# Self attention of a two-layer diffusion block: a pair addition of 128x2048 on GpSimd written as four additions of 128x512, with TensorE waiting for them head by head

## The chip, the cores and the metric

One core of one Trainium2 chip runs the whole program. The metric is the device time of one execution in microseconds (us). PE is TensorE, PEld its weight loads, DVE VectorE, ACT ScalarE, POOL GpSimd and SP the engine that issues most DMAs.

## The reference, cut to what matters

The input is `x` of 8 batches with 512 tokens of 512 features. Layer L0 adds a cross attention to a context of 77 tokens. Layer L1 adds a self attention, a second cross attention and an MLP with a hidden size of 2048. There are 16 heads of 32 features, all in float32. The change lies in the self attention:

```
attn_w = softmax(einsum('bhqd,bhkd->bhqk', q, k) * scale, axis=-1)
attn_out = einsum('bhqk,bhkd->bhqd', attn_w, v)   # then heads side by side
x = x + gate_a * (attn_out @ W_proj + b_proj)
```

## The kernel before, in words

The stages follow one another: preparation, cross attention L0, the products for queries, keys and values, self attention, the second cross attention, the MLP. Each engine has its own list of instructions, and semaphores tie the lists together. Steps of several loops are woven into one list by `braid`, so the order on each engine is fixed when the program is built.

The self attention works on 32 groups n, one for each batch and each set of four heads. In a group, `attend` makes the scores with keys on the partitions: 4 key tiles (kt) times 4 heads, one matmul each (L1901). ScalarE writes the exponential of each score tile (L1979) into `self_exponentials`, four buffers `p[0]` to `p[3]` of 128 x 4 heads x 512 queries in float32. TensorE then does two things with them. `values` (L1923) multiplies each `p[kt]` with the values, four matmuls with 32 columns, one for each head, into the four 32-partition strips of one bank. `sum_pair` (L1935) multiplies with a matrix of ones in the same four strips and gives the denominators. To halve those sums GpSimd first adds `p[1]` into `p[0]`, and `p[3]` into `p[2]` (L1781). So there are two additions for a group, 64 in all, and 64 calls of `sum_pair`.

TensorE asks for the sums late: `sum_pair(n, 0)` is called just before the values of kt 3, in the second step of the next group, and `sum_pair(n, 1)` just before the values of kt 1 of the next group. ScalarE may overwrite `p[0]` and `p[2]` only after the sums have read them (L1971, L1972).

Between these, TensorE makes the scores once more with queries on the partitions for group n+2 (L1880). VectorE takes the negated maximum of each (L1815), TensorE turns the maxima (L1889), and they go back as rows of the query stack. These maxima use three banks, so TensorE waits for VectorE when it is late. VectorE also does `finish` for the group before: it turns the sums (L1829), inverts them (L1832), spreads them (L1835), multiplies the heads (L1841: two inputs in SBUF) and takes the low part (L1846: two inputs in SBUF). In the groups 0 to 3 VectorE splits one piece of the projection weights as well (L266: `weight_stage` minus its high part, two inputs in SBUF). GpSimd adds the residual base (L1764) and the gated rows (L1790) for the batch before, tiles of 128x512.

From the group 27 on, steps of the second cross attention are woven in: its normalisation (L312, L321), transposes (L354) and the splits of its weights (L266).

A wait on TensorE is carried by the weight load of the matmul that follows it. `Port` leaves out a wait for a value that the engine has waited for already. In the cross attentions `values` has the four value matmuls (L1332), then a wait for VectorE's `sums_turned` of the group before, then the four sum matmuls (L1339).

Of the kernel before, what the change touches and what calls it, by code (L numbers as in the profile page):

```python
# [7 lines left out]
ALU = mybir.AluOpType  # L8
# [7 lines left out]
GH = P // HD  # L16
# [35 lines left out]
def s_at(kb):  # L52
    return S_AT + int(kb * KB)


class Done:


    def __init__(self, sem, base, by):
        self.sem, self.base, self.by = sem, base, by  # L60
# [1553 lines left out]
class SelfAttention:  # L1614
# [4 lines left out]
    def __init__(self, k, w, x_in, x_out, wp):  # L1619
        self.k, self.w, self.x_in, self.x_out, self.wp = k, w, x_in, x_out, wp  # L1620
        n, c = LAST, k.count
        self.key_ones = c("vector_self_key_ones", 4)
        self.q_fetched, self.k_fetched = k.slots("self_query_stack", 4, n, 3), k.slots("self_key_stack", 4, n, 3)
        self.v_loaded = k.slots("self_values", 3, n)
        self.smax, self.negmax = c("tensor_scores_for_max", n * GH * NT), c("vector_negated_maxima", n * GH * NT)
        self.rows_turned = c("tensor_turned_maxima", n)
        self.row_hi, self.row_lo = c("scalar_max_row_hi", n), c("vector_max_row_lo", n)
        self.rows_put = k.slots("self_max_rows", 4, n, 2)
        self.score, self.exp = c("tensor_scores_by_key", n * NT * GH), c("scalar_exponentials", n * NT * GH)
        self.av, self.summed = c("tensor_value_sums", n * NT), c("tensor_exponential_sums", n * 2)  # L1630
        self.paired = c("pool_exponential_pairs", n * 2)
        self.heads_copied, self.heads_hi = c("scalar_heads_float32", n), c("scalar_heads_hi", n)
        self.sums_turned, self.inverted = c("vector_sums_turned", n), c("vector_reciprocals", n)
        self.spread, self.normalised = c("vector_reciprocals_spread", n), c("vector_normalised_heads", n)
        self.heads_lo = c("vector_heads_lo", n)
        self.x_loaded, self.x_stored = c("dma_x_rows", B, 16), c("dma_x_out", B, 16)
        self.gate_loaded = c("dma_self_gate", B, 32)
        self.based, self.projected = c("pool_residual_bases", B * NT), c("tensor_projections", B * NT)
        self.gated, self.added = c("vector_gated_rows", B * NT), c("pool_residuals", B * NT)
        self.scores, self.max_banks, self.products = k.ring(0, 1), k.ring(2, 3, 4), k.ring(5)  # L1640
        self.heads, self.sums = k.ring(6), k.ring(7)
        self.q = [k.at(f"self_query_stack{i}", [ST_MAX, GH, N], s_at(at), F32R) for i, at in enumerate((0, 16, 80, 48))]
        self.keys = [k.at(f"self_key_stack{i}", [ST_MAX, GH, N], s_at(at + 8), F32R) for i, at in enumerate((0, 16, 80, 48))]
        self.p = [k.at(f"self_exponentials{i}", [P, GH, N], s_at(at)) for i, at in enumerate((32, 40, 64, 72))]
        self.w_p = k.pair("self_w_p", [P, KC, D], s_at(96), s_at(104))
        self.v = [k.at(f"self_values{i}", [P, NT, P], at) for i, at in enumerate((s_at(114), s_at(112), OUTS + 8 * KB))]
        self.gated_rows = k.at("self_gated_rows", [P, D], OUTS + 10 * KB)
        self.gate = k.at("self_gate_and_bias", [P, 2, D], WIDE)
# [108 lines left out]
    def gpsimd(self, e, pool):  # L1757
        k = self.k

        def add_base(b):  # L1760
            pool.wait_ge(*self.x_loaded(b))
            pool.wait_ge(*self.gate_loaded(b))
            for t in range(NT):
                e.tensor_tensor(k.x[:, t, :], k.x[:, t, :], self.gate[:, 1, :], ALU.add).then_inc(self.based.sem, 1)  # L1764

        def attend(n):
            for kt in range(NT):
                for h in range(GH):
                    yield
                    if h == 1:  # L1770
                        if kt:
                            values(n, kt - 1)
                        elif n:
                            values(n - 1, NT - 1)

        def values(n, kt):
            if kt % 2 == 0:
                return
            pool.wait_ge(*self.exp((n * NT + kt) * GH + GH - 1))
            pool.wait_ge(*self.av(n * NT + kt - 1))  # L1780
            e.tensor_tensor(self.p[kt - 1][:], self.p[kt - 1][:], self.p[kt][:], ALU.add).then_inc(self.paired.sem, 1)  # L1781

        def project(b):
            for t in range(NT):
                i = b * NT + t
                for _ in range(3):
                    yield
                pool.wait_ge(*self.gated(i))
                pool.wait_ge(*self.based(i))
                e.tensor_tensor(k.x[:, t, :], self.gated_rows[:], k.x[:, t, :], ALU.add).then_inc(self.added.sem, 1)  # L1790
                yield

        return SelfSteps(add_base=add_base, attend=attend, project=project, values=values)

    def vector(self, e, dve):
# [71 lines left out]
    def tensor(self, e, pe):  # L1867
# [59 lines left out]
        def sum_pair(n, j):  # L1927
            if j == 0:
                _, before = self.sums.take(("sums", n), self.sums_turned(n))
                if before:  # L1930
                    pe.wait_ge(*before)
            bk = self.sums.of["sums", n]
            pe.wait_ge(*self.paired(2 * n + j))
            for h in range(GH):
                mm = e.matmul(k.bank[h * HD:(h + 1) * HD, bk, :], k.ones[:], self.p[2 * j][:, h, :],  # L1935
                              start=j == 0, stop=j == 1)
            mm.then_inc(self.summed.sem, 1)

        def project(b):
            for t in range(NT):  # L1940
# [9 lines left out]
                yield  # L1950

        return SelfSteps(maxima=maxima, max_rows=max_rows, attend=attend, project=project, values=values, sum_pair=sum_pair)

    def scalar(self, e, act):
        k = self.k

        def max_rows(n):
            act.wait_ge(*self.rows_turned(n))
            if n >= 2:
                act.wait_ge(*self.rows_put(n - 2))  # L1960
            else:
                for done in self.freed_rows:
                    act.wait_ge(*done)
            e.activation(k.mr[n % 2][:, 0, :], k.bank[0:GH * NT, self.max_banks.of["rows", n], 0:P],
                         ACT.Copy).then_inc(self.row_hi.sem, 1)
            yield

        def attend(n):
            for kt in range(NT):
                if n > 0:  # L1970
                    act.wait_ge(*self.paired(2 * (n - 1) + kt // 2))  # L1971
                    act.wait_ge(*(self.av((n - 1) * NT + kt) if kt % 2 else self.summed(2 * (n - 1) + kt // 2)))  # L1972
                else:
                    for done in self.freed_p[kt // 2]:
                        act.wait_ge(*done)
                for h in range(GH):
                    i = (n * NT + kt) * GH + h
                    act.wait_ge(*self.score(i))
                    e.activation(self.p[kt][:, h, :], k.bank[:, self.scores.of["score", i], :], ACT.Exp,  # L1979
                                 scale=SCALE).then_inc(self.exp.sem, 1)  # L1980
                    yield

        def finish(n):
            yield
            yield
            act.wait_ge(*self.av(n * NT + NT - 1))
            if n >= 2:
                act.wait_ge(*self.heads_lo(n - 2))
            else:
                for done in self.freed_wide:  # L1990
                    act.wait_ge(*done)
            e.copy(k.o_wide[n % 2][:], k.bank[:, self.heads.of["heads", n], :]).then_inc(self.heads_copied.sem, 1)
            for _ in range(12):
                yield
            act.wait_ge(*self.normalised(n))
            if n >= 6:
                act.wait_ge(*self.projected(((n - 6) // G) * NT + NT - 1))
            else:
                for done in self.freed_o:
                    act.wait_ge(*done)  # L2000
            e.copy(k.o[n % 6][:, 0, :], k.o_wide[n % 2][:]).then_inc(self.heads_hi.sem, 1)
            yield

        return SelfSteps(lambda p: self.w.split_hi(e, act, p), max_rows=max_rows, attend=attend, finish=finish)


# [390 lines left out]
```

## Time and profile before

| | |
|---|---|
| median of three runs | 2545.93 us (2542.42 to 2553.8) |
| the profiled execution | 2551.88 us, its span 2550.1 us |
| PE busy | 2408.3 us, 94% of the span |
| DVE busy | 1390.8 us, 55% |
| ACT busy | 1025.2 us, 40% |
| POOL busy | 582.4 us, 23% |
| L1781 busy | 294.5 us in 64 instructions, mean 4602 ns |
| self attention | from about 822 to about 1476 us of the span |

Busy time of an engine is the union of its instructions. An idle time is put down to the instruction whose semaphore ended it, or to "issue" where no semaphore did. A float32 matmul stands in the trace as two matmuls, two passes of one instruction. So one `sum_pair` gives eight L1935 matmuls.

### The profile page before, as it was taken

To read this page: it belongs to the slowest core of one execution; us is meant where nothing else is said; L and a number is where in the kernel's file an instruction comes from. 1 tells how busy PE (TensorE), PEld (TensorE's weight loads), DVE (VectorE), ACT (ScalarE), POOL (GpSimd) and SP (SyncE) were. 2 spreads that over 40 slices of the span, in tenths; PEclk is the share of its full clock that TensorE was granted. 3 is DMA by queue.
4 is the path that set the end of the run, shared out by engine and by line. 5 is a ranking of instruction groups with operands and counts; after the bars stand their busy time and mean duration, and the time that the engine had idled before them with its cause. 6 is when DMAs were issued, how large, how long until landed. Compare 5 with 4: busy or idle time off the path is not lost.

```text
span 2550.1 us, 32330 instructions
## 1 busy us (share of the span) xinstructions
PE 2408.3 (94%) x12048; PEld 1688.5 (66%) x12048; DVE 1390.8 (55%) x2463; ACT 1025.2 (40%) x1831; POOL 582.4 (23%) x325
## 2 busy tenths in 40 slices
PE   6889999999999899999998789999999999999999
PEld 5656666578877344444444457667588888888887
DVE  4566666654456777877777457666643222322221
ACT  3444444433322555555554334444442322233232
POOL 2101211210000466666665412111211011101100
PEclk9889999999999899999999899999999999999999
DMA  6687767555574546565553478787431101110110
GB/s 209 188 208 225 210 188 216 174 168 194 190 239 150 120 114 157 138 149 136 124 148 92 127 184 218 202 222 194 153 108 58 58 1 58 58 51 7 58 42 17
DMA packets 261323, 354.19 MB, mean 139 GB/s; under 512 B 61027, under 2 KB 109243, under 8 KB 261166
## 3 DMA queue, kind: packets, MB, share of 16 engines
q1 hardware_dynamic: 259998, 348.27, 48.4%
q0 software_dynamic: 1168, 3.85, 0.4%
q8 instruction: 96, 1.57, 0.3%
q14 instruction: 61, 0.50, 0.1%
HBM read 233.78 MB, written 116.69 MB: 137 GB/s over the span
## 4 chain that ended last, share of the span: by engine, by line
PE 81%; DVE 7%; ACT 4%; issue 3%; DMA 3%; SPq 1%; POOL 1%; DVEq 0%; ACTq 0%; POOLq 0%
PE banks L396 43%; PE banks L2195 14%; PE banks L1901 6%; PE banks L1923 4%; PE banks L1880 4%; PE banks L1935 2%; PE banks L1318 2%; PE banks L1332 2%; PE banks L1339 2%; PE banks L354 2%; DMA norm_x<-x 1%; ACT wide L377 1%; DVE negated_max L1815 1%; DVE norm_x L321 1%; PE banks L765 1%
## 5 line engine op out<-in xcount | busy, mean ns | idle before, releaser
L1979 ACT ACTIVATE self_exponentials<-banks 128x512 f32<-128x512 f32 x512 | 286.4, 594 | 291.2 <-PE banks L1935 138.7
L1815 DVE TENSOR_REDUCE negated_max<-banks 128x1 f32<-128x512 f32 x512 | 329.9, 677 | 100.4 <-PE banks L1880 98.9
L1781 POOL TENSOR_TENSOR self_exponentials<-self_exponentials,self_exponentials 128x2048 f32<-128x2048 f32 x64 | 294.5, 4602 | 202.5 <-ACT self_exponentials L1979 202.5
L2195 PE MATMUL banks<-mlp_w_down_hi,out_parts 128*128 128x512 f32 x1024 | 333.8, 389 | 0.1
L337 POOL TENSOR_SCALAR norm_rstd<-norm_mean_var 128x4 f32<-128x4 f32 x32 | 8.0, 249 | 1341.3 <-DVE norm_mean_var L316 1341.3
L2152 DVE TENSOR_TENSOR out_parts<-wide,out_parts 128x512 fp32r<-128x512 f32 x128 | 93.0, 727 | 371.2 <-ACT out_parts L2224 371.2
L2214 ACT ACTIVATE wide<-banks,bias_columns 128x512 f32<-128x512 f32 x128 | 88.3, 690 | 426.0 <-PE banks L396 426.0
L1901 PE MATMUL banks<-self_query_stack,self_key_stack 98*128 98x512 f32 x512 | 233.3, 457 | 7.8 <-ACT self_exponentials L1979 4.9
L1901 PEld LDWEIGHTS banks<-self_query_stack,self_key_stack 98*128 98x128 f32 x512 | 97.6, 191 | 185.9 <-ACT self_exponentials L1979 147.3
L2195 PEld LDWEIGHTS banks<-mlp_w_down_hi,out_parts 128*128 128x128 f32 x1024 | 192.2, 188 | 40.5 <-DVE cross_last_x_rows L1261 0.5
L1880 PE MATMUL banks<-self_key_stack,self_query_stack 96*128 96x512 f32 x512 | 208.6, 411 | 6.3 <-DVE negated_max L1815 5.1
L2195 PE MATMUL banks<-mlp_w_down_lo,out_parts 128*128 128x512 f32 x512 | 199.2, 389 | 0.0
L1217 DVE TENSOR_REDUCE negated_max<-banks 128x4 f32<-128x308 f32 x256 | 121.1, 473 | 107.7 <-PE banks L396 104.0
L1923 PE MATMUL banks<-self_exponentials,self_values 128*32 128x512 f32 x1024 | 138.3, 612 | 0.7 <-ACT self_exponentials L1979 0.7
L1400 ACT ACTIVATE cross_exponentials<-banks 77x512 f32<-77x512 f32 x128 | 75.6, 592 | 111.7 <-PE banks L1318 111.6
L377 ACT ACTIVATE wide<-banks,modulation_columns 128x512 f32<-128x512 f32 x96 | 74.5, 776 | 108.8 <-PE banks L354 102.0
L1880 PEld LDWEIGHTS banks<-self_key_stack,self_query_stack 96*128 96x128 f32 x512 | 98.8, 193 | 25.3 <-DVE negated_max L1815 12.3
L312 DVE BATCH_NORM_STATS2 norm_stats<-norm_x 128x6 f32<-128x512 f32 x128 | 84.6, 671 | 53.7 <-DMA norm_x<-x 53.7
L1400 ACT ACTIVATE L_exponentials<-banks 77x512 f32<-77x512 f32 x128 | 75.3, 591 | 91.3 <-PE banks L1318 91.3
L2195 PEld LDWEIGHTS banks<-mlp_w_down_lo,out_parts 128*128 128x128 f32 x512 | 96.1, 188 | 19.9
L1592 ACT ACTIVATE out_parts<-banks,bias_columns 128x512 fp32r<-128x512 f32 x64 | 44.1, 689 | 161.3 <-PE banks L396 134.8
L329 DVE TENSOR_TENSOR x_lo<-wide,x_hi 128x512 fp32r<-128x512 f32 x80 | 56.3, 704 | 94.0 <-ACT x_hi L379 93.8
(208 smaller groups left out, 5323.6 us busy)
## 6 DMA issues: line engine op xcount, KB each, us to landing
L_query_stack<-q_parts_L SPq DMA_DIRECT2D x96, 256.0 KB, 4.9
norm_x<-x SPq DMA_DIRECT2D x24, 1024.0 KB, 7.5
self_query_stack<-q_parts_self SPq DMA_DIRECT2D x96, 256.0 KB, 4.1
self_key_stack<-k_parts_self SPq DMA_DIRECT2D x96, 256.0 KB, 6.3
cross_query_stack<-q_parts_cross SPq DMA_DIRECT2D x96, 256.0 KB, 4.9
x_rows<-x SPq DMA_DIRECT2D x23, 1024.0 KB, 5.9
x<-x_rows SPq DMA_DIRECT2D x22, 1024.0 KB, 5.0
q_parts_L<-out_parts SPq DMA_DIRECT2D x32, 512.0 KB, 3.7
```

Source lines behind the costliest of these rows:

```text
L377: e.activation(k.wides[w][:], bank, ACT.Identity, **kw).then_inc(self.wide.sem, 1)
L396: mm = e.matmul(out_ap, l, r, start=i == 0, stop=i == len(terms) - 1)
L1217: e.tensor_reduce(k.nm[n % 2][:, t:GH * NT:NT], k.bank[:, bk, 0:GH * S].rearrange("p (h k) -> p h k", k=S), AX_X, ALU.max, negate=True).th ...
L1400: e.activation(self.p[:, i % self.HEADS_KEPT, :], k.bank[0:S, self.scores.of["score", i], :], ACT.Exp, scale=SCALE).then_inc(self.exp.sem, 1)
L1781: e.tensor_tensor(self.p[kt - 1][:], self.p[kt - 1][:], self.p[kt][:], ALU.add).then_inc(self.paired.sem, 1)
L1815: e.tensor_reduce(k.nm[n % 2][:, h * NT + t:h * NT + t + 1], k.bank[:, self.max_banks.of["max", i], :], AX_X, ALU.max, negate=True).then_i ...
L1880: e.matmul(k.bank[:, bk, :], self.q[n % 4][0:ST, h, t * P:(t + 1) * P], self.keys[n % 4][0:ST, h, :], start=True, stop=True).then_inc(self ...
L1901: e.matmul(k.bank[:, bk, :], self.keys[n % 4][0:ST_MAX, h, kt * P:(kt + 1) * P], self.q[n % 4][0:ST_MAX, h, :], start=True, stop=True).the ...
L1923: mm = e.matmul(k.bank[h * HD:(h + 1) * HD, bk, :], self.v[n % 3][:, kt, h * HD:(h + 1) * HD], self.p[kt][:, h, :], start=kt == 0, stop=kt ...
L1979: e.activation(self.p[kt][:, h, :], k.bank[:, self.scores.of["score", i], :], ACT.Exp, scale=SCALE).then_inc(self.exp.sem, 1)
L2152: e.tensor_tensor(h[:, 1, :], k.wides[k.wide_turns.of["up", i]][:], raw(h[:, 0, :]), ALU.subtract).then_inc(self.lo.sem, 1)
L2195: mm = e.matmul(bank, l, w, start=j == 0 and q == 0, stop=j == JC - 1 and q == 2)
```

## The change

GpSimd's one addition over all four heads becomes four, one for each head, each with an increment of the same semaphore. TensorE's one wait ahead of the four sum matmuls becomes a wait ahead of each. ScalarE's wait is moved to the new count and still asks for the last head.

```diff
-        self.paired = c("pool_exponential_pairs", n * 2)
+        self.paired = c("pool_exponential_pairs", n * 2 * GH)
...
             pool.wait_ge(*self.exp((n * NT + kt) * GH + GH - 1))
             pool.wait_ge(*self.av(n * NT + kt - 1))
-            e.tensor_tensor(self.p[kt - 1][:], self.p[kt - 1][:], self.p[kt][:], ALU.add).then_inc(self.paired.sem, 1)
+            for h in range(GH):
+                e.tensor_tensor(self.p[kt - 1][:, h, :], self.p[kt - 1][:, h, :], self.p[kt][:, h, :],
+                                ALU.add).then_inc(self.paired.sem, 1)
...
-            pe.wait_ge(*self.paired(2 * n + j))
             for h in range(GH):
+                pe.wait_ge(*self.paired((2 * n + j) * GH + h))
                 mm = e.matmul(k.bank[h * HD:(h + 1) * HD, bk, :], k.ones[:], self.p[2 * j][:, h, :],
                               start=j == 0, stop=j == 1)
...
-                    act.wait_ge(*self.paired(2 * (n - 1) + kt // 2))
+                    act.wait_ge(*self.paired((2 * (n - 1) + kt // 2) * GH + GH - 1))
```

## Rows read from the trace of the kernel before

**Rows 1.** The page's chain that ended last, by engine
```profile
PE 81%; DVE 7%; ACT 4%; issue 3%; DMA 3%; SPq 1%; POOL 1%; DVEq 0%; ACTq 0%; POOLq 0%
```

**Rows 2.** Windows: length, then PE, PEld, DVE, ACT, POOL busy; clock, DMA share, GB/s
```profile
1179.00:1252.30 73.30, 72.24 (x376) 34.75 (x372) 56.22 (x92) 39.81 (x77) 47.71 (x17) 1.00 0.57 137
...
845.70:850.50 4.80, 4.63 (x16) 1.70 (x17) 3.40 (x7) 2.03 (x4) 0.00 (x0) 0.64 0.49 106
```

**Rows 3.** Source view of L1781: count, then shortest, median and longest in ns
```profile
L1781 POOL TENSOR_TENSOR self_exponentials<-self_exponentials,self_exponentials x64: 4502/4584/5012, 833.3 to 1447.1; 128x2048 f32<-128x2048 f32 x64
```

**Rows 4.** Timeline, one group of sum matmuls, in two narrow windows
```profile
1202.33 0.64 PE L1935 MATMUL banks<-self_exponentials,ones 128*32 128x512 f32 x4
...
1202.78 0.61 PE L1935 MATMUL banks<-self_exponentials,ones 128*32 128x512 f32 x4
```

**Rows 5.** Timeline of the cross attentions, sums (L1339) behind values (L1332)
```profile
158.08 0.13 PEld L1339 LDWEIGHTS banks<-L_exponentials,ones 77*32 77x32 f32 x4 [0.30 <-issue]
158.50 1.04 PE L1339 MATMUL banks<-L_exponentials,ones 77*32 77x512 f32 x8
...
384.03 0.16 PEld L1339 LDWEIGHTS banks<-L_exponentials,ones 77*32 77x32 f32 x8 [1.66 <-ACT wide L377]
...
1821.02 0.61 PE L1339 MATMUL banks<-cross_exponentials,ones 77*32 77x512 f32 x4
```

**Rows 6.** Timeline, a late addition and the sums that read it
```profile
1233.65 4.62 POOL L1781 TENSOR_TENSOR self_exponentials<-self_exponentials,self_exponentials 128x2048 f32<-128x2048 f32 x1
...
1241.70 1.06 PE L1935 MATMUL banks<-self_exponentials,ones 128*32 128x512 f32 x8
```

**Rows 7.** GpSimd additions of 128x512, a VectorE operation beside them, its source view
```profile
1206.84 1.28 POOL L1764 TENSOR_TENSOR x_rows<-x_rows,self_gate_and_bias 128x512 f32<-128x512 f32 x1 [0.57 <-DMA self_gate_and_bias<-gate_rows]
1207.47 1.20 DVE L1841 TENSOR_TENSOR heads_float<-heads_float,sums_turned 128x512 f32<-128x512 f32 x1
1208.08 1.73 POOL L1764 TENSOR_TENSOR x_rows<-x_rows,self_gate_and_bias 128x512 f32<-128x512 f32 x1
...
1452.15 5.39 POOL L1764 TENSOR_TENSOR x_rows<-x_rows,self_gate_and_bias 128x512 f32<-128x512 f32 x4 [0.55 <-DMA self_gate_and_bias<-gate_rows]
...
L1841 DVE TENSOR_TENSOR heads_float<-heads_float,sums_turned x32: 669/693/1321, 857.8 to 1455.4; 128x512 f32<-128x512 f32 x32
```

**Rows 8.** Timeline of the second head group, around a weight split (L266)
```profile
840.03 4.54 POOL L1781 TENSOR_TENSOR self_exponentials<-self_exponentials,self_exponentials 128x2048 f32<-128x2048 f32 x1 [2.13 <-ACT self_exponentials L1979]
840.56 4.57 DVE L266 TENSOR_TENSOR self_w_p_lo<-weight_stage,self_w_p_hi 128x512 fp32r<-128x512 f32 x1 [0.17 <-ACT self_w_p_hi L260]
...
845.79 0.28 PE L1889 MATMUL banks<-identity,negated_max 128*16 128x128 f32 x1 [2.49 <-DVE negated_max L1815]
```

**Rows 9.** Timeline, starts of the first sums of head groups 0, 3 and 4
```profile
840.71 1.06 PE L1935 MATMUL banks<-self_exponentials,ones 128*32 128x512 f32 x8
...
901.07 0.64 PE L1935 MATMUL banks<-self_exponentials,ones 128*32 128x512 f32 x4
...
917.40 1.07 PE L1935 MATMUL banks<-self_exponentials,ones 128*32 128x512 f32 x8
```

**Rows 10.** Timeline at the thirtieth head group
```profile
1358.92 4.77 DVE L321 TENSOR_SCALAR norm_x<-norm_x,norm_mean_var,norm_rstd 128x512 f32<-128x512 f32 x1
...
1364.34 0.79 PE L1880 MATMUL banks<-self_key_stack,self_query_stack 96*128 96x512 f32 x1 [4.63 <-DVE negated_max L1815]
```

**Rows 11.** Timeline, a split of the next stage's weights
```profile
1393.30 2.33 DVE L266 TENSOR_TENSOR cross_w_q_lo<-weight_stage,cross_w_q_hi 128x512 fp32r<-128x512 f32 x1
```

**Rows 12.** Timeline of a steady group: normalisation, then score matmul
```profile
1225.97 1.15 DVE L1841 TENSOR_TENSOR heads_float<-heads_float,sums_turned 128x512 f32<-128x512 f32 x1
...
1227.87 0.47 PE L1880 MATMUL banks<-self_key_stack,self_query_stack 96*128 96x512 f32 x1
```

**Rows 13.** Timeline, the last addition and its sums
```profile
1447.09 4.51 POOL L1781 TENSOR_TENSOR self_exponentials<-self_exponentials,self_exponentials 128x2048 f32<-128x2048 f32 x1 [10.37 <-ACT self_exponentials L1979]
...
1451.65 1.94 PE L1935 MATMUL banks<-self_exponentials,ones 128*32 128x512 f32 x8 [3.52 <-POOL self_exponentials L1781]
```

## Prediction

> **What bounds the kernel now.** I read the page first. Its chain that ended last is TensorE for 81% and GpSimd for 1% [rows 1]. Then the windows of the self attention: in one steady batch of four head groups TensorE is busy for 72.24 of 73.30 us at a granted clock of 1.00, and GpSimd for 47.71 us [rows 2]. So a shorter or longer addition is worth nothing by itself. It counts where TensorE waits for it, or where it holds up somebody for whom TensorE waits. The first is seen in the timeline of L1781 and L1935, the second in VectorE's timeline beside L1781.
>
> **Who waits for the addition.** An addition takes 4584 ns at the median [rows 3]. One of the late ones starts at 1233.65, ends at 1238.27, and its sums start at 1241.70: 3.4 us to spare [rows 6]. Of all 64 the steady groups' have 3.4 us or more, the first 2.8, and only the last has nothing: it ends at 1451.60, and its sums start at 1451.65 after 3.52 us of waiting [rows 13]. Starting the sums by the head therefore gains nothing in 63 of 64 places.
>
> **The four additions.** The same engine adds tiles of 128x512 in L1764. Without company one takes 1.28 us, and the next starts 1.24 us after it [rows 7]. Four give 3 x 1.24 + 1.28 = 5.0 us. The four with one collision took 5.39 us [rows 7]. So each pair takes 5.0 to 5.9 us in place of 4.58, 0.4 to 1.3 us more, and that lies within what they have to spare: 0 on the path. For the last pair I take +0.5 us (bounds +0.4 and +1.3), as TensorE has nothing else to do there.
>
> **Three more waits on TensorE for each sum, 192 in all.** Their values have been reached 1.5 us or more before TensorE comes, since the last piece ends at most 1.3 us later than now. What does a satisfied wait cost between matmuls in column strips? The passes of the four heads run side by side: four matmuls at 1202.33, four at 1202.78, eight in 0.9 us [rows 4]. If a wait broke this, the group would take longer. The cross attentions have such a wait between L1332 and L1339. There the four weight loads of L1339, the first of which carries the wait, start at 158.08, while the second passes of L1332 begin, and the matmuls at 158.50, 0.42 us on, like any pass [rows 5]. Of the 64 such groups, from 158 to 1821 us, 50 look like this. The others had to wait, as at 384.03, and even then all eight loads go within 0.16 us [rows 5]. I take 0 for the 192 waits. The upper bound, were the heads to run one after another, is a rival below.
>
> **Where the addition holds up VectorE.** This is the term that decides. VectorE's weight split L266 starts at 840.56, during an addition of 840.03 to 844.57, and takes 4.57 us, until 845.13, which is 0.56 us after the addition's end [rows 8]. A second operation with two SBUF inputs, L1841, takes 0.67 us alone [rows 7]. Started at 1207.47 beside an L1764 that ends at 1208.12 it takes 1.20, until 1208.67: again 0.55 after the end. The L1764 behind it starts at 1208.08, yet takes 1.73 us [rows 7]. So the two engines exclude each other for a whole instruction, and VectorE gets in between two GpSimd instructions that follow without a gap. Behind pieces of 1.28 us it waits for 1.3 us at most, not 4.6.
> The Trainium skill (SBUF — State Buffer, section "SBUF: two separate sides") calls the shared ports an exclusive lock, held for the full instruction; the trace agrees, 4.57 us against 0.67. By that rule too the wait falls to the rest of one piece, and the sum is the same.
>
> **Groups 1 to 3.** L266 falls into an addition three times. TensorE then idles for 2.49 us before L1889, once VectorE comes to its maxima [rows 8], and afterwards the clock is low: 0.64 over 4.80 us, a loss of 0.36 x 4.80 = 1.7 us [rows 2]. Together 4.2 a time. A second way to size it: from the sums of group 0 to those of group 3 it is 901.07 - 840.71 = 60.36 us, 20.1 a group, and the next group, which has neither weights to split nor projections, takes 917.40 - 901.07 = 16.33 [rows 9]. The excess is 60.36 - 3 x 16.33 = 11.4 us. With pieces the split ends at about 841.9 in place of 845.13, before TensorE runs dry (843.3, from 845.79 less 2.49). I take -10.5, as VectorE keeps 1.3 us of each wait and the split itself. Bounds: -11.4, and -7.5 where the clock falls in spite of it (3 x 2.49).
>
> **Group 29.** L321, a normalisation of one SBUF input, starts at 1358.92 beside an addition and takes 4.77 us, and TensorE idles for 4.63 us until 1364.34 [rows 10]. With pieces this first L321 ends some 3 us earlier, but the next two can meet further pieces. I take -3.0, bounds -2 and -5.5 (the idle time and some of the low clock behind it). Another L266 takes 2.33 us [rows 11], up to 1.0 less; the normalisation sets the pace there, and I take -0.6, bounds 0 and -1.
>
> **Where it costs.** In each of 7 batches an L1841 starts at the end of an addition: at 1225.97, 1.15 us, until 1227.12, so it waited for an end at about 1226.57 and ran 0.55. With pieces the addition ends 0.4 later, and so does L1841. Behind it stands a maximum for whose bank L1880 at 1227.87 waits [rows 12]. I take +0.35 each, 7 x 0.35 = +2.4, bounds 0 and +2.9. Other VectorE work of two SBUF inputs lies 1 us or more behind an addition's end.
>
> **Sum.** -10.5 - 3.0 - 0.6 + 2.4 + 0.5 = -11.2 us. The profiled execution goes from 2551.88 (span 2550.1 and 1.8 around it) to 2540.7. It lay 6 us above the median of the runs, 2545.93, so against the runs I expect 2534.7, said as 2534.5. By the bounds the main case is -17.5 to -5.3, that is 2528 to 2541.
>
> **Rivals.**
> *Satisfied waits break the strips (slower).* If the wait of the next head lets it start only behind the second pass of the head before, the eight passes form five steps in place of two, 3 x 0.44 = 1.3 us more a sum, 64 x 1.3 = +84 us, 2630; one head after another is 6 x 0.44 = 2.6, +169. It decides from 0.2 us a sum on. For it: no row has a wait inside a group of four. Against it: the load with the wait in L1339 goes ahead of unfinished passes. The Trainium skill (TensorE: Matmul & The Clock Gate, "Part 3: Packing small matmuls") holds that matmuls start and end strictly in program order; taken literally with heads written one by one this is the rival's +84, and the trace, four first passes ahead of four second ones, does not bear it out. Chance 0.05.
> *The gain is taken by the next wait (no change).* At 841 to 846 exponentials, maxima rows or the DMA fetches could come just behind, so that only 1 us each is won: -3 - 1 + 2.9 + 0.5, nothing to be seen, 2545. For it: VectorE still has its three pending maxima to do at once. Against it: group 4 runs at 16.33 with the same work. Chance 0.10.
> *GpSimd doesn't let go between pieces (no change).* Its next piece starts 0.04 us before the last ends, so the lock could pass on: 0 for the stalls, +2.9 and +0.5, 2549. Against it: L1841 beside L1764. Chance 0.05.
>
> **How the numbers follow.** Main case 0.80. A measurement of this kernel tells about 0.5%, 12.7 us, from no change. The main case's middle is 1.5 us short of that, so I give 0.34 of its 0.80 to faster and 0.46 to the same. With 0.15 of the two null rivals, and 0.01 of mishaps on either side: faster 0.35, same 0.59, slower 0.06. The range goes from 2525 (the low bound less the spread of the runs) to 2550 (the null rivals).
>
> **What would show it.** Right: L1781 x256 at about 1.28 us, L266 at 840 us under 2 us, no idle time before L1889 near 845, the clock at 1.00 there, sums of groups 0 to 3 some 16.5 us apart, L1935 unchanged at 0.9 us a group, L1841 in the projecting groups at 1.5 us. Wrong: L1935's passes spread over more than 1 us; L266 still at 4.5; a low clock at 847 without L266; or a new idle time of TensorE in the steady groups.

## The result

The changed kernel takes 2534.76 us at the median of 8 runs (2527.35 to 2540.86), the kernel before 2546.01 us at the median of 8 beside them (2541.22 to 2558.12). The ratio is 0.9952 with a 95% interval of 0.9931 to 0.9973: faster by 0.48%, just inside the 0.5% that I had set as the bound of a change. 2534.5 was predicted. The medians differ by 11.25 us where 11.2 was forecast; the interval reaches from 6.9 to 17.6 us, so that the two agree to the tenth is luck.

From the page of the changed kernel, the chain that ended last by engine, and the group of the addition, which answers to [rows 1] and [rows 3]:

```profile
PE 81%; DVE 8%; ACT 4%; issue 3%; DMA 2%; SPq 1%; POOL 1%; ACTq 0%; DVEq 0%; POOLq 0%
...
L1782 POOL TENSOR_TENSOR self_exponentials<-self_exponentials,self_exponentials 128x512 f32<-128x512 f32 x256 | 323.7, 1293 | 176.1 <-ACT self_exponentials L1981 176.1
```

GpSimd is busy for longer with the additions, 323.7 us in place of 294.5, and TensorE is as ever four fifths of the chain. What changed is in VectorE's timeline. The second head group in the changed kernel, VectorE, GpSimd and TensorE (start in us, duration in us, engine, line), against [rows 8]:

```profile
834.06 1.28 POOL L1782 TENSOR_TENSOR self_exponentials<-self_exponentials,self_exponentials 128x512 f32<-128x512 f32 x1 [1.67 <-ACT self_exponentials L1981]
834.59 1.30 DVE L266 TENSOR_TENSOR self_w_p_lo<-weight_stage,self_w_p_hi 128x512 fp32r<-128x512 f32 x1 [0.17 <-ACT self_w_p_hi L260]
835.82 1.27 DVE L1817 TENSOR_REDUCE negated_max<-banks 128x1 f32<-128x512 f32 x2
836.93 0.40 PE L1882 MATMUL banks<-self_key_stack,self_query_stack 96*128 96x512 f32 x1
837.16 0.27 PE L1891 MATMUL banks<-identity,negated_max 128*16 128x128 f32 x1
```

The first piece ends at 835.34. The weight split L266, which had waited for the whole addition and taken 4.57 us, ends at 835.89, 0.55 us after the piece. VectorE is at its maxima (L1817, before L1815) from 835.82 on, TensorE finds the one it needs, and L1891 (before L1889) follows without idle time, where it had waited for 2.49 us.

Windows of the changed kernel, one behind that place and one steady batch (length, busy PE, PEld, DVE, ACT, POOL, clock, DMA share, GB/s), against [rows 2]:

```profile
839.00:843.80 4.80, 4.80 (x30) 1.92 (x33) 3.93 (x7) 1.99 (x4) 2.07 (x3) 1.00 1.06 205
1172.50:1246.00 73.50, 71.85 (x372) 34.48 (x371) 56.62 (x92) 39.40 (x76) 50.54 (x40) 1.00 0.57 136
```

The granted clock is 1.00 behind the place, not 0.64: TensorE no longer stops there, and the clock no longer falls to its lower level, 1.2 GHz. The two windows of a steady batch are 73.50 and 73.30 us wide, about a batch each; by the first score matmuls of the groups 20 and 24 a batch takes 73.94 us, 73.28 before. The first sums of the groups 0, 3 and 4, against [rows 9]:

```profile
834.73 1.06 PE L1937 MATMUL banks<-self_exponentials,ones 128*32 128x512 f32 x8
...
883.35 0.64 PE L1937 MATMUL banks<-self_exponentials,ones 128*32 128x512 f32 x4
...
899.92 0.64 PE L1937 MATMUL banks<-self_exponentials,ones 128*32 128x512 f32 x4
```

Three groups in 883.35 - 834.73 = 48.62 us, 16.21 each, as long as a group without a stall; before they took 60.36.

The loss in the projecting groups, against [rows 12]. GpSimd's last piece, L1843 (before L1841) and the score matmul behind it:

```profile
1210.18 1.28 POOL L1782 TENSOR_TENSOR self_exponentials<-self_exponentials,self_exponentials 128x512 f32<-128x512 f32 x1
1210.44 1.58 DVE L1843 TENSOR_TENSOR heads_float<-heads_float,sums_turned 128x512 f32<-128x512 f32 x1
1212.77 0.47 PE L1882 MATMUL banks<-self_key_stack,self_query_stack 96*128 96x512 f32 x1 [0.53 <-DVE negated_max L1817]
```

L1843 waits for the last piece, which ends at 1211.46, and takes 1.58 us in place of 1.15. TensorE, which had not stopped there, waits 0.53 us for the maximum behind it. This happens in six of the seven batches. The seventh L1843 that waits for a last piece stands at 1361.82 and takes 1.58 us too, but the last L1882 of the stage starts at 1362.67, before this L1843 is done, so no L1882 waits behind it. Group 29, against [rows 10]:

```profile
1344.76 1.53 DVE L321 TENSOR_SCALAR norm_x<-norm_x,norm_mean_var,norm_rstd 128x512 f32<-128x512 f32 x1
...
1346.95 0.50 PE L1882 MATMUL banks<-self_key_stack,self_query_stack 96*128 96x512 f32 x1 [1.44 <-DVE negated_max L1817]
```

L321 takes 1.53 us in place of 4.77, and TensorE idles for 1.44 in place of 4.63. And the last sums, against [rows 13], now in four steps of a head (first and last step):

```profile
1430.72 1.05 PE L1937 MATMUL banks<-self_exponentials,ones 128*32 128x512 f32 x2 [0.29 <-POOL self_exponentials L1782]
...
1434.37 1.05 PE L1937 MATMUL banks<-self_exponentials,ones 128*32 128x512 f32 x2 [0.17 <-POOL self_exponentials L1782]
```

In the kernel before, the last sums end 6.5 us behind the start of the last values (L1923 at 1447.06): 4.5 of them are the whole addition, and 1.94 the eight passes at the low clock. Here it is 6.1 us, the four pieces and then the last head's 1.05 us: three heads are summed while GpSimd still adds, and the granted clock is 1.00 in these steps (1431 to 1434.4), not 0.50.

**The time, place by place.** I cut the self attention at the first score matmul by key of each head group and at the end of VectorE's last gated product (L1860, L1862 after). All of it takes 645.73 us in the profiled execution after, 657.46 before: 11.7 less. By place: group 0 -0.2, groups 1 to 3 -3.8, -4.0 and -4.0 (19.53, 20.16 and 20.18 become 15.73, 16.20 and 16.20), the six groups 6, 10, 14, 18, 22 and 26 with the wait behind a late L1843 +0.45 each (2.7 in all), group 29 -2.6, group 30 -0.8, from the start of group 31 to the end +0.45; all others lie within 0.3 of nothing and come to +0.5 together. What follows the stage takes 1071.7 us against 1071.1. The two profiled executions differ by 16.8 us, as the stages ahead of the self attention, whose work is the same, were 5.8 us shorter in the second. In the nine traces of this document they take 815.8 to 821.6 us, though no kernel differs there. So this is spread between runs, and the comparisons below leave it out by going by the stage as well as by the timed runs.

### The profile page after: what moved, and what is told of

It is laid out like the page before. It is cut to its first block, busy times and chain, and to the rows that moved or that the text cites. A ratio compares the mean times of both kernels' runs of the same rounds, so it can differ in the third digit from the quotient of the medians.

```text
span 2533.3 us, 32522 instructions
## 1 busy us (share of the span) xinstructions
PE 2404.1 (95%) x12048; PEld 1683.0 (66%) x12048; DVE 1381.0 (55%) x2463; ACT 1025.1 (40%) x1831; POOL 610.7 (24%) x517
## 4 chain that ended last, share of the span: by engine, by line
PE 81%; DVE 8%; ACT 4%; issue 3%; DMA 2%; SPq 1%; POOL 1%; ACTq 0%; DVEq 0%; POOLq 0%
PE banks L396 43%; PE banks L2197 14%; PE banks L1903 5%; PE banks L1925 4%; PE banks L1882 4%; PE banks L1937 2%; PE banks L1318 2%; PE banks L1339 2%; PE banks L1332 2%; PE banks L354 2%; DVE negated_max L1817 1%; DMA norm_x<-x 1%; ACT wide L377 1%; DVE heads_float L1843 1%; DVE heads_float L1245 1%
## 5 line engine op out<-in xcount | busy, mean ns | idle before, releaser
L1817 DVE TENSOR_REDUCE negated_max<-banks 128x1 f32<-128x512 f32 x512 | 329.8, 677 | 96.8 <-PE banks L1882 95.4
L1782 POOL TENSOR_TENSOR self_exponentials<-self_exponentials,self_exponentials 128x512 f32<-128x512 f32 x256 | 323.7, 1293 | 176.1 <-ACT self_exponentials L1981 176.1
L1882 PE MATMUL banks<-self_key_stack,self_query_stack 96*128 96x512 f32 x512 | 206.7, 407 | 6.9 <-DVE negated_max L1817 6.7
L1882 PEld LDWEIGHTS banks<-self_key_stack,self_query_stack 96*128 96x128 f32 x512 | 97.8, 191 | 24.3 <-issue 8.2
```

Source lines behind the costliest of these rows:

```text
L1782: e.tensor_tensor(self.p[kt - 1][:, h, :], self.p[kt - 1][:, h, :], self.p[kt][:, h, :], ALU.add).then_inc(self.paired.sem, 1)
L1817: e.tensor_reduce(k.nm[n % 2][:, h * NT + t:h * NT + t + 1], k.bank[:, self.max_banks.of["max", i], :], AX_X, ALU.max, negate=True).then_i ...
L1882: e.matmul(k.bank[:, bk, :], self.q[n % 4][0:ST, h, t * P:(t + 1) * P], self.keys[n % 4][0:ST, h, :], start=True, stop=True).then_inc(self ...
```

## The experiments

All kernels in one table; each was timed against the kernel before on one chip in turns, and the stage is that of its one profiled execution. The kernel before had medians of 2546.01, 2547.29 and 2545.99 us in the three rounds of runs; each ratio is to that of its own round. A projecting group is one of the six with the wait behind the late L1841. The edits, what was expected and what follows stand below it.

| kernel | median us | ratio to before, 95% | self attention us | groups 1 to 3 us | projecting group us |
|---|---|---|---|---|---|
| before | 2546.01 | 1 | 657.5 | 19.5, 20.2, 20.2 | 20.86 |
| the change | 2534.76 | 0.9952 (0.9931 to 0.9973) | 645.7 | 15.7, 16.2, 16.2 | 21.30 |
| one wait | 2531.61 | 0.9942 (0.9920 to 0.9963) | 646.3 | 15.7, 16.2, 16.2 | 21.28 |
| pieces at the stalls | 2533.13 | 0.9950 (0.9931 to 0.9969) | 642.7 | 15.7, 16.2, 16.2 | 20.87 |
| pieces elsewhere | 2551.21 | 1.0018 (1.0003 to 1.0033) | 660.2 | 20.7, 21.1, 18.7 | 21.28 |
| splits moved | 2533.39 | 0.9952 (0.9934 to 0.9971) | 646.2 | 15.7, 16.2, 16.2 | 20.85 |
| both | 2531.51 | 0.9945 (0.9923 to 0.9967) | 643.3 | 15.7, 16.2, 16.2 | 21.28 |
| halves | 2533.60 | 0.9947 (0.9926 to 0.9968) | 647.0 | 15.9, 16.5, 16.5 | 20.99 |
| all together | 2526.25 | 0.9928 (0.9911 to 0.9946) | 638.6 | 15.7, 16.2, 16.2 | 20.85 |

The intervals overlap among the faster kernels, so the timed runs place them against the kernel before and not against each other. The stage does that, but only where the work repeats: groups like 4, 7 and 8 and, for the same kind of addition, the projecting ones repeat within 0.05 us from run to run. The groups just ahead of the projecting ones take 18.2 to 19.0 us in any kernel. Group 30 takes 28.2 us where the granted clock is 1.00 in it and 29.2 to 30.1 where it is 0.94. The stretch from the start of group 31 to the end takes 67.8 to 69.1 us in the four kernels that leave the last addition whole. So a difference of 1 us in the whole stage says nothing by itself.

### One wait for the four pieces

```diff
+            pe.wait_ge(*self.paired((2 * n + j) * GH + GH - 1))
             for h in range(GH):
-                pe.wait_ge(*self.paired((2 * n + j) * GH + h))
                 mm = e.matmul(k.bank[h * HD:(h + 1) * HD, bk, :], k.ones[:], self.p[2 * j][:, h, :],
```

> The changed kernel, but TensorE waits once, for the last head's piece, ahead of the four sum matmuls, as it did before. Theory (satisfied waits are free, the gain is VectorE's): the same as the changed kernel, 2535 us, self attention from the first score matmul by key to the last gated row 645.7 us as in the changed kernel, and the first seven matmul starts of a sum to its last still 0.47 us; only the last sum may differ, by under 0.5 us. Rival (each wait costs TensorE something, and the gain would be larger without it): 0.01 us for each of 192 waits would give 2 us less, 0.05 us would give 10 us less, 2525.

The groups without a meeting are as long as with four waits (16.18 us against 16.18 to 16.20; a further kernel with four waits below, with the splits moved as well, has 16.17 to 16.18), the stage 646.3 against 645.7, half a microsecond of it from group 31 on. There the eight passes wait 3.94 us for the last piece and then take 1.93 at the low clock: the last sums end 6.9 us behind the start of the last values, not 6.1. This is the one place where the wait by the head is worth something. One sum and the values behind it, from the timeline of this kernel:

```profile
1181.40 1.07 PE L1937 MATMUL banks<-self_exponentials,ones 128*32 128x512 f32 x8
1182.29 1.04 PE L1925 MATMUL banks<-self_exponentials,self_values 128*32 128x512 f32 x8
```

The values follow 0.89 us after the sums, and so they do in the changed kernel (834.73 to 835.62) and before. In the changed kernel the first and the last start of the eight passes are 0.473 us apart in the median of the 64 sums, here too. That the waits are there shows in the changed kernel's trace too: the weight loads of the second, third and fourth head each carry one, 7 ns apart. The 192 additional waits cost TensorE nothing that can be seen.

### Pieces only where a stall was seen, and the counterpart

```diff
+        self.pieces = [GH if (i < 3 or i >= 28) and (i, j) != (n - 1, 1) else 1 for i in range(n) for j in range(2)]
...
+            w = GH // self.pieces[2 * n + kt // 2]
+            for h in range(0, GH, w):
+                e.tensor_tensor(self.p[kt - 1][:, h:h + w, :], self.p[kt - 1][:, h:h + w, :], self.p[kt][:, h:h + w, :],
+                                ALU.add).then_inc(self.paired.sem, 1)
```

> Four pieces only for the additions of the groups 0 to 2 and 28 to 31 without the very last one; whole additions in the groups 3 to 27 and for the last. Theory: the groups 1 to 3 keep their gain (15.7 to 16.2 us each in place of 19.5 to 20.2), the seven groups that lost 0.45 us each get it back (20.85 in place of 21.30), the last addition its 0.45: self attention 645.7 - 3.2 - 0.45 = 642.1 us, the whole 2531 us. Rival (pieces everywhere are what gains, for instance by sums that start earlier): only 13 of 64 additions are in pieces, so most of the gain is gone, 2543 us, self attention 655 us.

Thirteen of 64 additions in pieces keep all of the gain in the groups 1 to 3, and the projecting groups are back at 20.87 us. The stage is 642.7 us, 0.6 more than expected. Against the changed kernel the six projecting groups give back 2.6 us, where I had counted seven groups and 3.2; group 29 loses 2.4, by an accident that I come to below; group 30 and the stretch behind it are 1.1 and 1.4 us shorter, which is about what they vary by. The rival, a gain with the number of pieces, is out. The counterpart has the condition `3 <= i < 28`:

> The counterpart: four pieces only in the groups 3 to 27, whole additions elsewhere. Theory: no gain at all, and the loss of 7 x 0.45 = 3.2 us: groups 1 to 3 at 19.5 to 20.2 us, the projecting groups at 21.3, self attention 657.5 + 3.2 = 660.7 us, the whole 2549 us. Rival (pieces gain wherever they are): 50 of 64 additions in pieces give most of the gain, 2537 us.

Fifty additions in pieces gain nothing and lose 6 x 0.42 = 2.5 us; the seven of the expectation count one group too many here as well. It is the only kernel slower than before, by 0.18% with an interval that just leaves out no change; the stage gives 2.7 us. Its windows show what the clock adds to a stall (columns as above):

```profile
842.00:850.00 8.00, 7.84 (x23) 4.08 (x23) 5.09 (x10) 3.22 (x6) 0.68 (x1) 0.57 0.43 108
862.00:870.00 8.00, 6.69 (x20) 3.44 (x21) 5.25 (x9) 2.77 (x6) 0.10 (x1) 0.57 0.54 130
882.00:890.00 8.00, 5.49 (x27) 2.57 (x31) 7.25 (x11) 3.81 (x8) 2.00 (x2) 1.00 0.50 119
```

In all three groups L266 meets a whole addition and takes 4.4 to 4.6 us. In the groups 1 and 2 the clock is at its lower level for most of the 8 us behind (0.57), and they last 20.7 and 21.1 us. In the kernel before, with the same instructions there, it was 19.5 and 20.2: what the clock adds differs from run to run. In the third it stays at 1.00 and the group lasts 18.7: the 2.5 us of idle time alone above 16.2. So a stall of this size costs 2.5 us, and 1.3 (group 1 before, 3.8 - 2.5) to 2.5 more (group 1 here, 20.7 - 15.7 - 2.5) where the clock falls behind it.

### The weight splits moved out of the addition

```diff
             if n < G:
-                s.split(self.wp_at + n)
+                late = after(4, (s.split(self.wp_at + i) for i in (n,)))
...
-            side = []
+            side = [late] if n < G else []
```

> The kernel before with whole additions; only the four splits of the projection weights are put four steps later in their groups, in the gap between two additions. Theory (the stall is the meeting of a split and a whole addition): each L266 takes 0.7 us in place of 4.5, no idle time of TensorE before L1889, the clock stays at 1.00 at 847 us, groups 1 to 3 at 15.7 to 16.3 us: self attention 657.5 - 11.7 = 645.8 us, 2534 us, without a single piece. Rival (the pieces themselves, or the head-by-head waits, make groups 1 to 3 shorter): no gain, 2546 us, or a little more because the splits now stand beside other work.

This is the kernel before, with whole additions; both parts of the split move, ScalarE's high part (L260) too. The split's source view, and one of them in the timeline between two additions:

```profile
L266 DVE TENSOR_TENSOR self_w_p_lo<-weight_stage,self_w_p_hi x4: 692/692/693, 822.9 to 872.0; 128x512 fp32r<-128x512 f32 x4
...
833.76 4.58 POOL L1781 TENSOR_TENSOR self_exponentials<-self_exponentials,self_exponentials 128x2048 f32<-128x2048 f32 x1 [2.08 <-ACT self_exponentials L1979]
839.62 0.69 DVE L266 TENSOR_TENSOR self_w_p_lo<-weight_stage,self_w_p_hi 128x512 fp32r<-128x512 f32 x1
841.95 4.58 POOL L1781 TENSOR_TENSOR self_exponentials<-self_exponentials,self_exponentials 128x2048 f32<-128x2048 f32 x1 [3.61 <-ACT self_exponentials L1979]
```

All four splits take 0.69 us, the groups 1 to 3 are as short as with pieces, and the ratio of 0.9952 is the changed kernel's. The gain needs no piece: it is the meeting of a VectorE operation with a long GpSimd instruction that cost 11.7 us. With both cures at once:

> The changed kernel with the weight splits moved four steps later as well. Theory (both cures take away the same meeting, so they don't add up): groups 1 to 3 at 15.7 to 16.2 us as with either alone, self attention 645.2 to 646 us, 2534 us. Rival (pieces and moved splits act on different things): the sum of both gains, self attention 634 us, 2523 us.

The groups 1 to 3 are the same again, so the two don't add up. The stage is 2 us below what I expected: 1.0 of it in group 30, whose clock stays at 1.00 here, 0.8 behind it and 0.4 in group 0. The last belongs to the moved split: the three kernels that move it have a group 0 of 17.4 to 17.5 us, the six others 17.8 to 18.1. The first split meets no addition in any of them, but it stood ahead of maxima, and TensorE's idle time before L1889 there falls from 2.35 to 1.75 us.

### Two halves

```diff
-        self.paired = c("pool_exponential_pairs", n * 2 * GH)
+        self.pieces = [2 for i in range(n) for j in range(2)]
+        self.paired = c("pool_exponential_pairs", sum(self.pieces))
```

> Every addition in two pieces of two heads (128x1024) in place of four of one. Theory (VectorE waits for the rest of the piece that runs, and the addition's whole length decides whether it meets L1841): a half takes about 2.3 us, so L266 ends at about 1.7 us behind its start plus 0.55, still before TensorE runs dry: groups 1 to 3 at 15.7 to 16.3 us, a gain of 11.7 as with quarters. The addition takes 4.65 to 4.7 us in place of 4.97, so L1841 behind it ends 0.1 us later than with whole additions, not 0.4: the projecting groups at 20.95, not 21.30. Self attention 657.5 - 11.7 + 0.7 - 2.5 = 644 us, or less, the whole 2532 us. Rival (the gain goes with the number of pieces): half of it, groups 1 to 3 at 18 us, self attention 652 us, 2540 us.

Source views of the addition (L1787 here) and of the split:

```profile
L1787 POOL TENSOR_TENSOR self_exponentials<-self_exponentials,self_exponentials x128: 2337/2383/2893, 828.3 to 1433.9; 128x1024 f32<-128x1024 f32 x128
...
L266 DVE TENSOR_TENSOR self_w_p_lo<-weight_stage,self_w_p_hi x4: 679/2271/2394, 817.4 to 868.6; 128x512 fp32r<-128x512 f32 x4
```

A half takes 2.38 us, the splits 2.27 to 2.39, and the groups 1 to 3 gain 3.64 to 3.70 each, 11.0 of the 11.7. The projecting groups lose 0.14 us in place of 0.45. The missing 0.7 us goes with idle time of 0.42 us before L1896 (L1889 in the kernel before) in the groups 2 and 3: with halves the split ends a little too late for TensorE, with quarters it does not. The stage is 3 us above what I had expected: in group 29 L321 takes 2.6 us and the group comes out 0.7 us longer than before, not 2.5 shorter. There VectorE meets piece after piece, and TensorE needs it at once.

### All together

Whole additions up to group 27 with the splits moved, pieces from 28 on, and for the last pair no addition:

```diff
+            tiles = (2, 3) if (n, j) == (LAST - 1, 1) else (2 * j,)
+            for t in tiles:
+                for h in range(GH):
+                    if len(tiles) == 1:
+                        pe.wait_ge(*self.pair_done(2 * n + j, h))
+                    mm = e.matmul(k.bank[h * HD:(h + 1) * HD, bk, :], k.ones[:], self.p[t][:, h, :],
+                                  start=j == 0, stop=j == 1 and t == tiles[-1])
```

> What the runs point to: whole additions in the groups 0 to 27 with the splits moved; four pieces in the groups 28 to 31, where the normalisation of the next stage meets them; and for the very last pair no addition at all: TensorE sums the exponentials of both key tiles itself, eight more passes at the low clock in place of 3.5 us of waiting. Theory: groups 1 to 3 -11.7, group 0 -0.4, group 29 and 30 -3.4, the end -2 us: self attention 657.5 - 17.5 = 640 us, the whole 2529 us, 4 to 6 us below the changed kernel. Rival (the end is set by the next stage's loads, and the last sum is hidden): 642 us, 2531 us.

The last values and the sixteen passes of the last sums in the timeline:

```profile
1427.93 1.07 PE L1930 MATMUL banks<-self_exponentials,self_values 128*32 128x512 f32 x8 [0.46 <-ACT self_exponentials L1989]
1428.82 1.90 PE L1945 MATMUL banks<-self_exponentials,ones 128*32 128x512 f32 x16
```

I had counted on the low clock here. But TensorE doesn't stop, the granted clock is 1.00 from 1427.9 to 1430.8 (it was 0.50 from 1451.6 to 1453.6 in the kernel before), and sixteen passes take 1.90 us, about as long as the eight took at the low clock [rows 13]. From the start of group 31 to the end it is 65.6 us in place of 68.7. The stage is at 638.6 us, 18.8 below before and 7.1 below the change, and the whole at 2526.25, 0.72% faster than before. The timed runs alone don't set it apart from the changed kernel, as the intervals overlap; the stage does.

## Why the prediction was right

**The four additions** take 5.0 us without a collision, as worked out (4.94 to 5.88 over all), and their slack, 2.3 us or more, hides them in 63 of 64 places.

**The last pair** was taken at +0.5, and the stretch from group 31 on did get 0.45 us longer, but that is luck. At the sums themselves 0.5 us was won, 6.1 us in place of 6.5: the prediction took only the longer addition and left out that TensorE now sums three heads while it waits, and that its clock stays up. The other +0.9 us of the stretch lies before and behind the last sums, and it is within the 1.3 us by which this stretch varies in kernels that leave the last addition alone.

**The waits on TensorE** were taken as free, from the cross attentions; one wait in place of four changes nothing. The rival of +84 us is out. What the prediction took for a literal reading of the Trainium skill (TensorE: Matmul & The Clock Gate, "Part 3: Packing small matmuls"), where matmuls start and end in program order, doesn't lead to that rival: counted by instruction, the four heads' matmuls start at 834.734, 834.740, 834.747 and 834.754 in the changed kernel and their second passes at 835.187 to 835.207, each 7 ns behind the one before, so the trace agrees with the page, and heads that overlap break no such order.

**Where the addition holds up VectorE** was the term that decides, and moving the splits alone shows it. The groups 1 to 3 gave -11.7 us where -10.5 was taken and -11.4 was the bound. I had kept 0.9 us for the waits that remain, up to the rest of one piece. They cost nothing, since L266 now ends before TensorE asks. The other 0.3 is the bound's: it took 16.33 us for each group, and group 1 needs only 15.7. That the stall is 2.5 us of idle time and the rest the clock's, as the first way of sizing it had it, is shown by the group in which the clock did not fall. That the gain would be taken by the next wait (chance 0.10) is out: TensorE's idle time in the groups 2 and 3 is 0.57 us each, as in group 4.

**Group 29** gave -2.6 where -3.0 was taken, group 30 -0.8 where -0.6 was; there TensorE's longest wait (before L396) falls from 2.11 to 1.24 us at the same granted clock.

**Where it costs**: 6 x 0.45 = 2.7 us where 7 x 0.35 = 2.4 was taken, with 2.9 as the bound. The mechanism is the one described. Each was a little too low, since all of VectorE's 0.43 us reached TensorE, which has no slack there (0.53 us of idle time before L1882). And one was too many, since the seventh L1841 has no such matmul behind it. The expectations of the experiments, written with 7 x 0.45 = 3.2, repeat this miscount.

**The sum** of the stage is -11.7 where -11.2 was predicted. The groups 1 to 3 gave 1.2 us more than taken; the late L1841, group 29 and all that the sum didn't list (-0.2 in group 0, +0.5 in the others) took 1.0 us of it back. So the closeness is in part luck.

**GpSimd doesn't let go** was given 0.05 as a rival for every meeting. It does let go as a rule, but I found one meeting in which it didn't, below.

## What to carry to other kernels

Look for the longest GpSimd instruction that reads SBUF, and at the durations of VectorE's operations with two SBUF inputs beside it: a duration of several times the median is a wait, and where VectorE feeds TensorE it is a stall, with the clock on top. Here moving the few operations that met it was as good as cutting the instruction, and didn't lengthen it; cutting all instructions also cost something, where their end moved into the next meeting. And a wait whose value had long been reached stood between matmuls in column strips without breaking their overlap. Where the value has not been reached and TensorE has nothing else to do, as at the very last sums, waiting by the head pays.

## What the hardware showed that I had not expected

In the kernel with pieces at the stalls, at the start of group 29, GpSimd ran the four residual additions L1764 (L1768 there) with a VectorE operation waiting. Timelines of VectorE, GpSimd and TensorE:

```profile
1341.17 5.08 DVE L1848 TENSOR_TENSOR heads_float<-heads_float,sums_turned 128x512 f32<-128x512 f32 x1
...
1340.74 4.96 POOL L1768 TENSOR_TENSOR x_rows<-x_rows,self_gate_and_bias 128x512 f32<-128x512 f32 x4
...
1347.00 0.77 PE L1887 MATMUL banks<-self_key_stack,self_query_stack 96*128 96x512 f32 x1 [4.03 <-DVE negated_max L1822]
```

VectorE asked at 1341.17, during the first of the four, and got in only after the fourth, at 1345.70: it took 5.08 us, and TensorE idled for 4.03. In the changed kernel the same operation stands at the same place, 0.43 us behind the start of the first L1764, and takes 1.39 us. So between two GpSimd instructions that follow without a gap VectorE usually gets in, but nothing guarantees it. In the nine traces I count some 460 VectorE operations behind 800 us that end a fixed 0.55 us (L321: 0.29) behind the end of a GpSimd instruction, the mark of a wait. In about 290 of them a further GpSimd instruction stood right behind, and this is the only one that waited for that one too. What decides it stays open, and one trace doesn't tell how often it happens. It cost that kernel's group 29 the gain of the change, 2.4 us.

A GpSimd instruction that follows without a gap starts 0.03 to 0.06 us before the end of the one ahead of it. A VectorE operation that starts in this last moment waits for the whole of the next. The nine traces have some 75 of these, most of them L1846 (1.80 us in place of 0.67). The costly one is the normalisation of group 29 [rows 10]. The two GpSimd instructions around its start, in the kernel before:

```profile
1357.21 1.72 POOL L1764 TENSOR_TENSOR x_rows<-x_rows,self_gate_and_bias 128x512 f32<-128x512 f32 x1
1358.90 4.50 POOL L1781 TENSOR_TENSOR self_exponentials<-self_exponentials,self_exponentials 128x2048 f32<-128x2048 f32 x1
```

L321 starts at 1358.92, 0.01 us before the L1764 ends and 0.02 after the addition has begun, and waits for all 4.50 us of it. With pieces it meets the same end and waits for one piece.

The last is that L321 has one input in SBUF and two scalars for each partition, and still waits for a whole GpSimd addition just like an operation with two inputs: 4.77 us [rows 10], where the median of its 128 is 0.54.
